# Three parts of queries and keys stored once, and read back for the stacks in three pieces instead of two

## The chip, the cores and the metric

The kernel runs on one core of one Trainium2 chip. The metric is the device time of the whole program in microseconds; the median of three runs is compared. Engines are called PE (matrix products), DVE (vector), ACT (scalar, activation functions), POOL (GpSimd) and SP (the queue that issues most DMAs).

## What is computed

A residual stream x of 2048 tokens by 128 channels passes a gated cumulative-sum block, then a two-layer feed-forward block with attention and experts, then a plain attention block, then the same feed-forward block once more:

```python
x = x + attn_a(layernorm(x), ...)
x = x + ffn(layernorm(x), ...)      # 2 layers: causal attention, then experts
x = x + attn_b(layernorm(x), ...)   # 16 heads of 8, no mask
x = x + ffn(layernorm(x), ...)      # the same weights again

# in ffn, for layer l in (0, 1):
x = x + attn(ln(x), wq[l], wk[l], wv[l], wo[l], ...)
x = x + moe(ln(x), ...)             # l == 0: two of eight experts by token; l == 1: two for the sequence
# attention of either kind
q, k, v = split into 16 heads of 8 columns
scores = q @ k.T * 8 ** -0.5        # causal in ffn
out = softmax(scores) @ v
```

So there are five attentions in the program. They are called f0 and f1 (the two layers of the first feed-forward block), b (the plain one), and g0 and g1 (the second feed-forward block); the last letter of a tile's name in the trace is f, b or g.

## The kernel before

**Stacks.** Every query and key value is split into three bf16 parts, high, mid and low (numbered 0, 1, 2), so that a product of two fp32 numbers becomes a sum of products of bf16 parts. Six such products are taken in one matmul, whose contraction runs over 48 rows: six groups of eight rows, one group for each product, eight rows for the eight columns of a head. `q_stack` holds on its partitions the parts 0, 1, 2, 0, 0, 1 of the queries and `k_stack` the parts 2, 1, 0, 0, 1, 0 of the keys; the upper half of the partitions holds the same for the odd heads. The parts are made with channels on partitions, so they pass through DRAM (`q_parts`, `k_parts`) to be regrouped.

**Writes.** The tokens are cut into four chunks of 512 columns (`CHUNKS`, c = 0 to 3). For each chunk SP writes three parts of q and of k. `Q_SLOTS` and `K_SLOTS` say which part stands in which of the four groups of DRAM rows; part 0 stands in two, so its write moves 256 KB and the other two move 128 KB. Each write adds 16 to `written[k][c % 2]`.

**Loads.** `load_stacks` (`EarlyProjection.load` in f1 and g1) loads chunk c for half b of the partitions. It waits until the three writes of q, then of k, have landed (`written` at 16 * 3 for each second chunk), and issues two DMAs for each stack: 32 rows, then 16 rows of the same DRAM tensor again. So one call issues four DMAs, and there are eight calls for each attention, 40 in all, 160 DMAs. Of one attention's eight calls, those of half 0 are issued by SP. Those of half 1 come from ACT for chunk 0 and from POOL for chunks 1 to 3 (in f1 and g1 SP issues the one of chunk 0 as well).

**Where the calls stand.** In f0 and b (`project_qkv`) and g0 (`project_behind`) the projection runs directly before the attention. SP writes the high parts of chunk c and then calls `load_stacks(sp, c - 1, 0)`; ACT makes the high parts of chunk 1 and then calls `load_stacks(act, 0, 1)`, ahead of copying a later chunk and of its mid parts:

```python
                    if c >= 2:
                        act.wait_ge(written[k][c % 2], 16 * 3 * (c // 2))
...
                if c == 1:
                    load_stacks(act, 0, 1)
                if c + 2 < CHUNKS:
                    copy_chunk(c + 2)
```

The first two of these lines let the high parts of chunk 3 be made only when the writes of chunk 1 have landed, since they share a buffer. In g0 POOL runs `load_stacks(pool, 1, 1)` and then `first_rows.powers(pool, BACK, 2)`, whose result `rstd` (line 848) DVE needs to normalise the last rows. In f1 and g1 (`EarlyProjection`) the projection of chunks 0 to 2 is spread through the experts of the layer before. There SP loads chunk 0 and half 0 of chunk 1 between rows of combine weights, and POOL loads half 1 of chunk 1 between its multiplications.

**In the attention.** PE, DVE, ACT and SP follow orders that `Plan` writes out ahead of time. PE scans scores for the row maxima (lines 1681 and 1692), DVE reduces them (1841, 1843, 1848), and SP sends the maxima as a shift row into `q_stack` (1913). PE then makes scores again (1719), ACT takes the exponential (1789), POOL sets what lies above the diagonal to zero in the causal layers (`affine_select`, 1902), and PE multiplies by the values (1740). POOL's loop over the diagonal units k holds the late loads: with `late` = 0 in f0 and g0, and 12 in f1 and g1, chunk 2 is loaded ahead of select number `late` and chunk 3 four selects later:

```python
                if (k - late) % 4 == 0 and 0 <= (k - late) // 4 < CHUNKS - EARLY:
                    projected["load"](pool, EARLY + (k - late) // 4, 1)
```

Of the kernel before, what the change touches and what calls it, by code (L numbers as in the profile page):

```python
# [7 lines left out]
BF16 = mybir.dt.bfloat16  # L8
# [8 lines left out]
S = 2048  # L17
# [18 lines left out]

Q_SLOTS = [0, 1, 2, 0]
K_SLOTS = [2, 1, 0, 0]
SLOTS = len(Q_SLOTS)
Q_AGAIN, K_AGAIN = 0, 1  # L40
AGAIN = 2
STACK = (SLOTS + AGAIN) * HD
PAIRS = HEADS // 2
# [34 lines left out]
class Memory:  # L78
# [35 lines left out]
    def __init__(self, nc, ctx, ins):  # L114
# [48 lines left out]
        self.weights_split = ctx.enter_context(nc.semaphore("weights_split"))  # L163
        self.q_dram = nc.dram_tensor("q_parts", [SLOTS * HD, HEADS, S], BF16, kind="Internal").ap()
        self.k_dram = nc.dram_tensor("k_parts", [SLOTS * HD, HEADS, S], BF16, kind="Internal").ap()
        self.r_dram = nc.dram_tensor("inverse_sums", [HEADS, S], F32, kind="Internal").ap()
# [450 lines left out]
def project_qkv(nc, m, n, buffers, first=None, layer=None):  # L617
# [6 lines left out]
    with ExitStack() as ctx:  # L624
# [34 lines left out]
        def write_part(sp, c, k, part):  # L659

            dram, parts_of = ((m.q_dram, Q_SLOTS), (m.k_dram, K_SLOTS))[k]
            places = [g for g, of in enumerate(parts_of) if of == part]
            stride = places[1] - places[0] if len(places) > 1 else 1
            dst = dram.rearrange("(g d) h q -> (d h) g q", d=HD)[:, places[0]:places[-1] + 1:stride,
                                                               c * CH:(c + 1) * CH]
            sp.dma_start(dst, parts[:, c % 2, k, part:part + 1, :].broadcast_to([P, len(places), CH]))\
                .then_inc(written[k][c % 2], 16)

        def load_stacks(queue, c, b):

            cols = slice(c * CH, (c + 1) * CH)
            for k, (stack, dram, arrived, again) in enumerate(((m.q_stack, m.q_dram, m.q_in, Q_AGAIN),
                                                               (m.k_stack, m.k_dram, m.k_in, K_AGAIN))):
                queue.wait_ge(written[k][c % 2], 16 * 3 * (c // 2 + 1))
                if c == CHUNKS - 1:
                    queue.wait_ge(v_ready, CHUNKS)
                at = HALF * b
                for n, first in ((SLOTS, 0), (AGAIN, again)):
                    queue.dma_start(stack[at:at + n * HD, c, :, :],
                                    dram.rearrange("r (hp b) s -> r b hp s", b=2)[first * HD:(first + n) * HD, b, :, cols])\  # L680
                        .then_inc(arrived[b][c], 16)
                    at += n * HD
# [208 lines left out]
def project_behind(nc, m, n, buffers, layer, first_rows, attended, finish):  # L891

    src, end = m.x, CHUNKS - 1
    with ExitStack() as ctx:
# [26 lines left out]
        def write_part(sp, c, k, part):  # L921

            dram, parts_of = ((m.q_dram, Q_SLOTS), (m.k_dram, K_SLOTS))[k]
            places = [g for g, of in enumerate(parts_of) if of == part]
            stride = places[1] - places[0] if len(places) > 1 else 1
            dst = dram.rearrange("(g d) h q -> (d h) g q", d=HD)[:, places[0]:places[-1] + 1:stride,
                                                               c * CH:(c + 1) * CH]
            sp.wait_ge((high_ready, mid_ready, low_ready)[part], 2 * c + k + 1)
            sp.dma_start(dst, parts[:, c % 2, k, part:part + 1, :].broadcast_to([P, len(places), CH]))\
                .then_inc(written[k][c % 2], 16)  # L930

        def load_stacks(queue, c, b):

            cols = slice(c * CH, (c + 1) * CH)
            for k, (stack, dram, arrived, again) in enumerate(((m.q_stack, m.q_dram, m.q_in, Q_AGAIN),
                                                               (m.k_stack, m.k_dram, m.k_in, K_AGAIN))):
                queue.wait_ge(written[k][c % 2], 16 * 3 * (c // 2 + 1))
                if c == end:
                    queue.wait_ge(v_ready, CHUNKS)
                at = HALF * b  # L940
                for n, first in ((SLOTS, 0), (AGAIN, again)):
                    queue.dma_start(stack[at:at + n * HD, c, :, :],
# [169 lines left out]
class EarlyProjection:  # L1112
# [105 lines left out]
    def write(self, sp, c, k, part):  # L1218
        sp.wait_ge((self.high_ready, self.mid_ready, self.low_ready)[part], 2 * c + k + 1)
        dram, parts_of = ((self.m.q_dram, Q_SLOTS), (self.m.k_dram, K_SLOTS))[k]  # L1220
        places = [g for g, of in enumerate(parts_of) if of == part]
# [5 lines left out]
    def load(self, queue, c, b):  # L1227
        m, cols = self.m, slice(c * CH, (c + 1) * CH)
        if c == 2:
            queue.wait_ge(*self.ones_back)  # L1230
        for k, (stack, dram, arrived, again) in enumerate(((m.q_stack, m.q_dram, m.q_in, Q_AGAIN),
                                                           (m.k_stack, m.k_dram, m.k_in, K_AGAIN))):
            queue.wait_ge(self.written[k][c % 2], 16 * 3 * (c // 2 + 1))
            at = HALF * b
            for n, first in ((SLOTS, 0), (AGAIN, again)):
                queue.dma_start(stack[at:at + n * HD, c, :, :],
# [388 lines left out]
def attention_heads(nc, m, n, buffers, projected, finish, rows_of, raw_weights, w2, stale, early, first_rows=None):  # L1625
# [8 lines left out]
    for g, (_, _, _, tiles) in enumerate(groups):  # L1634
        shift_moves.append((2 if tiles == TPC else 4) + (shift_moves[g - 2] if g >= 2 else 0))
    arrived = 32 * (m.layers + 1)
    m.layers += 1
# [1180 lines left out]
```

## Time and profile before

| what | value |
|---|---|
| median of three runs | 3050.44 us (3050.01 to 3052.54) |
| the profiled execution | 3052.74 us, of which the span of instructions is 3051.0 us |
| PE busy | 2639.0 us (86%) |
| DVE busy | 2597.2 us (85%) |
| ACT busy | 2249.0 us (74%) |
| POOL busy | 637.2 us (21%) |
| DMA | 109883 packets, 119.09 MB, mean 39 GB/s |

Busy time is time in instructions that compute. Issuing a DMA isn't counted as busy, though it holds the engine's queue, so an engine that issues DMAs shows as idle in this table. Each share is one of the whole span.

### The profile page before, as it was taken

How to read it: one execution, taken by the hardware profiler on the slowest of the kernel's cores; microseconds unless marked ns; L12 is line 12 of the kernel's file. 1: busy time of each engine (PE TensorE's matmuls, PEld its weight loads, DVE VectorE, ACT ScalarE, POOL GpSimd, SP SyncE). 2: the span in 40 equal slices, each digit the busy share in tenths (PEclk: the TensorE clock that was granted, in tenths of full speed). 3: DMA queues.
4: the chain of work that ended last, by engine and by line, in shares of the span. 5: the costliest groups of instructions: out<-in, count | busy, mean ns of one | idle time of the engine just before them, and what ended most of it. 6: DMA issues, size and time to landing. Idle time of an engine off the chain costs nothing. (4 is left out here: it accounts for less than half of the span.)

```text
span 3051.0 us, 71491 instructions
## 1 busy us (share of the span) xinstructions
PE 2639.0 (86%) x28144; PEld 1156.1 (38%) x28144; DVE 2597.2 (85%) x3516; ACT 2249.0 (74%) x4330; POOL 637.2 (21%) x1175
## 2 busy tenths in 40 slices
PE   3579999899799995779999999599999998899976
PEld 3432333677323333422222223233333775323325
DVE  4679999788799995799999999599998887899976
ACT  1248988677489884459999999478988675688874
POOL 5233211434421011100000000132102543321011
PEclk8779999999799997879999999799999998899998
DMA  1051000214300000320000000420001224300001
GB/s 34 29 125 36 27 25 18 66 54 102 71 24 22 14 13 26 78 63 9 15 12 13 12 15 10 119 54 27 16 13 32 64 63 94 62 31 16 13 16 28
DMA packets 109883, 119.09 MB, mean 39 GB/s; under 512 B 20726, under 2 KB 87660, under 8 KB 109548
## 3 DMA queue, kind: packets, MB, share of 16 engines
q1 hardware_dynamic: 102444, 98.21, 12.0%
q0 software_dynamic: 4608, 13.96, 2.2%
q8 instruction: 222, 3.64, 0.5%
q10 hardware_dynamic: 2496, 2.36, 0.4%
q14 instruction: 113, 0.93, 0.1%
HBM read 70.31 MB, written 43.78 MB: 37 GB/s over the span
## 5 line engine op out<-in xcount | busy, mean ns | idle before, releaser
L1789 ACT ACTIVATE h_probsf<-h_ps_lowf 128x512 f32<-128x512 f32 (+3 forms) x812 | 424.4, 550 | 111.5 <-PE h_ps_lowf L1719 70.9
L1789 ACT ACTIVATE h_probsg<-h_ps_lowg 128x512 f32<-128x512 f32 (+3 forms) x812 | 424.4, 550 | 104.1 <-PE h_ps_lowg L1719 65.7
L1789 ACT ACTIVATE h_probsb<-h_ps_lowb 128x512 f32<-128x512 f32 x683 | 389.1, 596 | 61.0 <-PE h_ps_lowb L1719 46.0
L1740 PE MATMUL h_ps_valuesf<-h_probsf,v_all 128*9 128x256 f32 (+2 forms) x4608 | 350.7, 377 | 25.9 <-POOL h_probsf L1902 19.2
L1740 PE MATMUL h_ps_valuesg<-h_probsg,v_all 128*9 128x256 f32 (+2 forms) x4608 | 348.3, 375 | 26.2 <-POOL h_probsg L1902 19.2
L1740 PE MATMUL h_ps_valuesb<-h_probsb,v_all 128*9 128x256 f32 x4096 | 317.9, 382 | 7.8 <-ACT h_drainedb L1798 3.1
L1841 DVE TENSOR_REDUCE h_maxima_0b<-h_ps_scanb 128x2 f32<-128x1024 f32 x256 | 292.7, 1216 | 6.6 <-PE h_ps_scanb L1681 6.4
L1841 DVE TENSOR_REDUCE h_maxima_2b<-h_ps_scanb 128x2 f32<-128x1024 f32 x256 | 292.8, 1217 | 5.1 <-PE h_ps_scanb L1681 5.1
L1841 DVE TENSOR_REDUCE h_maxima_0f<-h_ps_scanf 128x2 f32<-128x1024 f32 x224 | 258.8, 1217 | 19.2 <-PE h_ps_scanf L1681 18.6
L1841 DVE TENSOR_REDUCE h_maxima_0g<-h_ps_scang 128x2 f32<-128x1024 f32 x224 | 258.6, 1217 | 18.6 <-PE h_ps_scang L1681 17.9
L1789 ACT ACTIVATE h_probsf<-h_ps_highf 128x512 f32<-128x512 f32 (+3 forms) x404 | 224.0, 554 | 35.1 <-PE h_ps_lowf L1719 32.5
L1789 ACT ACTIVATE h_probsg<-h_ps_highg 128x512 f32<-128x512 f32 (+3 forms) x404 | 224.0, 554 | 35.0 <-PE h_ps_lowg L1719 32.3
L1902 POOL TENSOR_SCALAR_AFFINE_SELECT h_probsg<-h_probsg 128x128 f32<-128x128 f32 (+1 forms) x384 | 121.5, 330 | 608.9 <-ACT h_probsg L1789 601.8
L1681 PE MATMUL h_ps_scanf<-k_stack,q_stack 48*128 48x512 bf16 (+3 forms) x1280 | 218.8, 362 | 27.7 <-DVE h_maxima_0f L1841 8.2
L1902 POOL TENSOR_SCALAR_AFFINE_SELECT h_probsf<-h_probsf 128x128 f32<-128x128 f32 (+1 forms) x384 | 121.5, 330 | 577.8 <-ACT h_probsf L1789 571.0
L1681 PE MATMUL h_ps_scang<-k_stack,q_stack 48*128 48x512 bf16 (+3 forms) x1280 | 218.4, 361 | 24.0 <-DVE h_maxima_0g L1841 7.4
L1719 PE MATMUL h_ps_lowf<-q_stack,k_stack 49*128 49x256 bf16 (+2 forms) x1368 | 227.7, 286 | 11.4 <-DMA q_stack<-h_shiftsf 5.5
L1719 PE MATMUL h_ps_lowg<-q_stack,k_stack 49*128 49x256 bf16 (+2 forms) x1368 | 226.8, 286 | 7.4 <-ACT h_probsg L1789 2.6
L1681 PE MATMUL h_ps_scanb<-k_stack,q_stack 48*128 48x512 bf16 x1024 | 202.8, 393 | 21.5 <-DVE h_maxima_0b L1841 9.4
L1789 ACT ACTIVATE h_probsb<-h_ps_highb 128x512 f32<-128x512 f32 x341 | 203.4, 596 | 11.2 <-PE h_ps_lowb L1719 8.4
L1719 PE MATMUL h_ps_lowb<-q_stack,k_stack 49*128 49x256 bf16 x1366 | 200.4, 275 | 5.9 <-ACT h_probsb L1789 5.6
L1841 DVE TENSOR_REDUCE h_maxima_2f<-h_ps_scanf 128x2 f32<-128x1024 f32 x160 | 185.5, 1219 | 14.3 <-PE h_ps_scanf L1681 13.4
(478 smaller groups left out, 5226.7 us busy)
## 6 DMA issues: line engine op xcount, KB each, us to landing
q_stack<-combine_weights SPq DMA_DIRECT2D x64, 256.0 KB, 3.7
q_stack<-in_L_ffn_e_w SPq DMA_DIRECT2D x24, 256.0 KB, 3.4
q_stack<-q_parts SPq DMA_DIRECT2D x22, 256.0 KB, 5.6
k_stack<-k_parts SPq DMA_DIRECT2D x22, 256.0 KB, 7.4
attended<-h_drainedf SPq DMA_DIRECT2D x16, 256.0 KB, 2.3
attended<-h_drainedf SPq DMA_DIRECT2D x32, 128.0 KB, 2.0
attended<-h_drainedb SPq DMA_DIRECT2D x32, 128.0 KB, 1.9
attended<-h_drainedg SPq DMA_DIRECT2D x16, 256.0 KB, 2.5
```

The source lines that it names most:

```text
L1681: last = nc.tensor.matmul(ps_scan[:, i % RING_A, b, at:at + width], m.q_stack[rows, c, 2 * quad + hp, t * P:(t + 1) * P], m.k_stack[rows, ...
L1719: last[b] = nc.tensor.matmul(ps_scores[(2 * n_pair + b) % RING_S][:, width * i + off:width * (i + 1)], m.k_stack[rows, kb // TPC, pair, at ...
L1740: last = nc.tensor.matmul(ps_values[32 * j:32 * j + VD, low:high], m.v_all[:, kb, QUAD * quad + j, :], probs[:, (u + j % banks) % RING_P, ...
L1789: nc.scalar.activation(by_head(probs[:, of % RING_P, :], of), by_head(ps_scores[of % RING_S], of), ACT.Exp, scale=SOFTMAX_SCALE).then_inc( ...
L1841: nc.vector.tensor_reduce(found[:, :, low], now, AXIS_X, ALU.max).then_inc(freed, 1)
L1902: nc.gpsimd.affine_select(out=at, in_=at, compare_op=ALU.is_ge, fill=0.0, base=0, pattern=[[0, at.shape[1]], [1, P]], channel_multiplier=- ...
```

## The change

Each part is written to DRAM once: `q_parts` and `k_parts` have three groups of eight rows instead of four. The stacks, which hold the same as before, are read in three pieces of 24, 8 and 16 rows. The numbers for which the attention waits follow from the count of pieces (48 for each layer instead of 32).

```diff
-Q_SLOTS = [0, 1, 2, 0]
-K_SLOTS = [2, 1, 0, 0]
-SLOTS = len(Q_SLOTS)
-Q_AGAIN, K_AGAIN = 0, 1
-AGAIN = 2
-STACK = (SLOTS + AGAIN) * HD
+Q_PARTS = [0, 1, 2]
+K_PARTS = [2, 1, 0]
+PARTS = len(Q_PARTS)
+Q_ROWS = ((0, 3), (0, 1), (0, 2))
+K_ROWS = ((0, 3), (2, 1), (1, 2))
+STACK = sum(n for _, n in Q_ROWS) * HD
...
-        self.q_dram = nc.dram_tensor("q_parts", [SLOTS * HD, HEADS, S], BF16, kind="Internal").ap()
-        self.k_dram = nc.dram_tensor("k_parts", [SLOTS * HD, HEADS, S], BF16, kind="Internal").ap()
+        self.q_dram = nc.dram_tensor("q_parts", [PARTS * HD, HEADS, S], BF16, kind="Internal").ap()
+        self.k_dram = nc.dram_tensor("k_parts", [PARTS * HD, HEADS, S], BF16, kind="Internal").ap()
...
         def write_part(sp, c, k, part):
 
-            dram, parts_of = ((m.q_dram, Q_SLOTS), (m.k_dram, K_SLOTS))[k]
+            dram, parts_of = ((m.q_dram, Q_PARTS), (m.k_dram, K_PARTS))[k]
             places = [g for g, of in enumerate(parts_of) if of == part]
...
-                for n, first in ((SLOTS, 0), (AGAIN, again)):
+                for first, n in parts_of:
                     queue.dma_start(stack[at:at + n * HD, c, :, :],
                                     dram.rearrange("r (hp b) s -> r b hp s", b=2)[first * HD:(first + n) * HD, b, :, cols])\
                         .then_inc(arrived[b][c], 16)
...
-    arrived = 32 * (m.layers + 1)
+    arrived = 16 * len(Q_ROWS) * (m.layers + 1)
```

The write and the load are changed alike in the three places where they are written out. The order of PE's and DVE's instructions doesn't change. Three places on the other queues show what does.

On SP, in the projection of f0, before: the writes of chunk 1's high parts, the load of chunk 0's half 0, and the first mid part of chunk 1. `128x2x512` is a write to two places.

```order
L666 DMA q_parts<-p_partsf 128x2x512
L666 DMA k_parts<-p_partsf 128x2x512
L679 DMA q_stack<-q_parts 32x8x512
L679 DMA q_stack<-q_parts 16x8x512
L679 DMA k_stack<-k_parts 32x8x512
L679 DMA k_stack<-k_parts 16x8x512
L666 DMA q_parts<-p_partsf 128x512
```

The same place of the changed kernel:

```order
L666 DMA k_parts<-p_partsf 128x512
L679 DMA q_stack<-q_parts 24x8x512
L679 DMA q_stack<-q_parts 8x8x512
L679 DMA q_stack<-q_parts 16x8x512
L679 DMA k_stack<-k_parts 24x8x512
L679 DMA k_stack<-k_parts 8x8x512
L679 DMA k_stack<-k_parts 16x8x512
L666 DMA q_parts<-p_partsf 128x512
```

The writes keep their number and those of the high parts lose half of their size; four loads become six, ahead of the next writes.

On ACT, in the projection of b: the call for chunk 0's half 1, between the high parts of chunk 1 (815) and the copy of chunk 3 (801).

```order
 L815 ACTIVATE p_partsb<-p_ps_mixedb 128x512 x2
-L679 DMA q_stack<-q_parts 32x8x512
+L679 DMA q_stack<-q_parts 24x8x512
+L679 DMA q_stack<-q_parts 8x8x512
 L679 DMA q_stack<-q_parts 16x8x512
-L679 DMA k_stack<-k_parts 32x8x512
+L679 DMA k_stack<-k_parts 24x8x512
+L679 DMA k_stack<-k_parts 8x8x512
 L679 DMA k_stack<-k_parts 16x8x512
 L801 ACTIVATE q_stack<-p_ps_turnb 128x512
```

Two issues more stand ahead of the copy.

On POOL, in the attention of f1: the two late loads among the selects.

```order
 L1248 DMA k_stack<-k_stack 1x16x512 x2
 L1902 AFFINE_SELECT h_probsf<-h_probsf 128x128 x4
-L1236 DMA q_stack<-q_parts 32x8x512
-L1236 DMA q_stack<-q_parts 16x8x512
-L1236 DMA k_stack<-k_parts 32x8x512
+L1236 DMA q_stack<-q_parts 24x8x512
+L1236 DMA q_stack<-q_parts 8x8x512
+L1236 DMA q_stack<-q_parts 16x8x512
+L1236 DMA k_stack<-k_parts 24x8x512
+L1236 DMA k_stack<-k_parts 8x8x512
 L1236 DMA k_stack<-k_parts 16x8x512
 L1902 AFFINE_SELECT h_probsf<-h_probsf 128x128 x4
```

Each of the two calls has six issues where it had four, and the selects behind it stand behind them.

## Rows read from the trace of the kernel before

**Rows 1.** The page: the span.

```profile
span 3051.0 us, 71491 instructions
```

**Rows 2.** DMA issues: tile, queue, count, KB each, median us to landing.

```profile
q_stack<-q_parts SPq DMA_DIRECT2D x22, 256.0 KB, 5.6
...
q_stack<-q_parts POOLq DMA_DIRECT2D x15, 256.0 KB, 4.7
```

**Rows 3.** By source line: ns of one issue, min/median/max, first and last start.

```profile
L1236 SPq DMA_DIRECT2D k_stack<-k_parts x20: 591/602/617, 712.1 to 2625.2; - x20
...
L1236 POOL DMA_DIRECT2D k_stack<-k_parts x12: 530/558/583, 736.6 to 2607.5; - x12
...
L1248 POOL DMA_DIRECT2D k_stack<-k_stack x4: 507/544/584, 800.4 to 2599.5; - x4
```

**Rows 4.** Timeline of f0's start: start us, us, engine, line; idle before and releaser.

```profile
150.00 1.27 ACTq L679 DMA_DIRECT2D k_stack<-k_parts  x2
...
151.37 0.78 ACT L803 ACTIVATE q_stack<-p_ps_turnf,vecs 128x512 f32<-128x512 f32 x1 [3.87 <-issue]
...
160.28 1.26 ACT L818 ACTIVATE p_partsf<-p_ps_qkf,vecs_dh 128x512 bf16<-128x512 f32 x2 [3.35 <-DMA q_parts<-p_partsf]
...
164.81 0.61 PE L1681 MATMUL h_ps_scanf<-k_stack,q_stack 48*128 48x128 bf16 x4 [8.18 <-issue]
```

**Rows 5.** Windows: PE, PEld, DVE, ACT, POOL busy, PEclk, DMA share, GB/s.

```profile
152.00:162.00 10.00, 4.64 (x21) 3.35 (x19) 6.63 (x16) 5.08 (x10) 1.49 (x3) 0.84 1.00 229
```

**Rows 6.** Timeline of b's projection.

```profile
1278.22 0.60 ACT L801 ACTIVATE q_stack<-p_ps_turnb 128x512 f32<-128x512 f32 x1 [2.31 <-issue]
...
1279.36 1.29 DVE L755 TENSOR_TENSOR p_partsb<-p_restb,p_partsb 128x512 bf16<-128x512 f32 x2 [2.46 <-ACT p_partsb L826]
...
1288.01 0.60 ACT L815 ACTIVATE p_partsb<-p_ps_mixedb 128x512 bf16<-128x512 f32 x1 [2.63 <-PE p_ps_mixedb L789]
```

**Rows 7.** The chain that ended last, in g0's projection: start us, us, what.

```profile
1943.27 7.89 DMA q_parts<-p_partsg
...
1951.45 1.16 POOL q_stack L942 x2
1952.61 1.09 POOL k_stack L942 x2
...
1953.72 1.04 POOL rstd L848
```

**Rows 8.** Timelines of f1 and g1: value matmuls behind POOL's late loads.

```profile
807.33 0.41 PE L1740 MATMUL h_ps_valuesf<-h_probsf,v_all 128*9 128x128 f32 x8 [1.54 <-POOL h_probsf L1902]
...
810.59 1.04 PE L1740 MATMUL h_ps_valuesf<-h_probsf,v_all 128*9 128x256 f32 x8 [1.02 <-POOL h_probsf L1902]
...
2605.91 0.41 PE L1740 MATMUL h_ps_valuesg<-h_probsg,v_all 128*9 128x128 f32 x8 [1.52 <-POOL h_probsg L1902]
...
2609.18 1.04 PE L1740 MATMUL h_ps_valuesg<-h_probsg,v_all 128*9 128x256 f32 x8 [1.12 <-POOL h_probsg L1902]
```

**Rows 9.** Timeline of f0 behind POOL's second late load.

```profile
187.14 1.53 POOL L1902 TENSOR_SCALAR_AFFINE_SELECT h_probsf<-h_probsf 128x128 f32<-128x128 f32 x6
...
188.06 0.62 PE L1740 MATMUL h_ps_valuesf<-h_probsf,v_all 128*9 128x256 f32 x8
```

**Rows 10.** Timeline of the experts ahead of f1, behind POOL's load.

```profile
738.38 1.29 POOL L2312 TENSOR_TENSOR q_stack<-q_stack 128x512 f32<-128x512 f32 x1 [0.67 <-ACT q_stack L2643]
```

**Rows 11.** Timeline of f0: the first score matmul.

```profile
181.34 0.61 PE L1719 MATMUL h_ps_lowf<-q_stack,k_stack 49*128 49x512 bf16 x2 [4.15 <-DMA q_stack<-h_shiftsf]
```

**Rows 12.** DMA from 798 to 802 us: packets of SP's queue; issues.

```profile
q1 hardware_dynamic: 32, 0.00, 0.7%
...
q_stack<-h_shiftsf SPq DMA_DIRECT2D x2, 2.0 KB
```

**Rows 13.** Windows in f1, columns as in rows 5.

```profile
804.00:808.00 4.00, 2.46 (x41) 1.08 (x39) 2.00 (x4) 1.72 (x6) 3.99 (x10) 1.00 0.68 143
808.00:812.00 4.00, 2.60 (x34) 1.07 (x30) 2.44 (x2) 2.34 (x5) 2.93 (x9) 0.65 1.07 173
```

More of the change, by code:

```diff
@@ L671, in load_stacks @@
             cols = slice(c * CH, (c + 1) * CH)
-            for k, (stack, dram, arrived, again) in enumerate(((m.q_stack, m.q_dram, m.q_in, Q_AGAIN),
-                                                               (m.k_stack, m.k_dram, m.k_in, K_AGAIN))):
+            for k, (stack, dram, arrived, parts_of) in enumerate(((m.q_stack, m.q_dram, m.q_in, Q_ROWS),
+                                                               (m.k_stack, m.k_dram, m.k_in, K_ROWS))):
                 queue.wait_ge(written[k][c % 2], 16 * 3 * (c // 2 + 1))
@@ L921, in write_part @@
         def write_part(sp, c, k, part):
-            dram, parts_of = ((m.q_dram, Q_SLOTS), (m.k_dram, K_SLOTS))[k]
+            dram, parts_of = ((m.q_dram, Q_PARTS), (m.k_dram, K_PARTS))[k]
             places = [g for g, of in enumerate(parts_of) if of == part]
@@ L934, in load_stacks @@
             cols = slice(c * CH, (c + 1) * CH)
-            for k, (stack, dram, arrived, again) in enumerate(((m.q_stack, m.q_dram, m.q_in, Q_AGAIN),
-                                                               (m.k_stack, m.k_dram, m.k_in, K_AGAIN))):
+            for k, (stack, dram, arrived, parts_of) in enumerate(((m.q_stack, m.q_dram, m.q_in, Q_ROWS),
+                                                               (m.k_stack, m.k_dram, m.k_in, K_ROWS))):
                 queue.wait_ge(written[k][c % 2], 16 * 3 * (c // 2 + 1))
@@ L940, in load_stacks @@
                 at = HALF * b
-                for n, first in ((SLOTS, 0), (AGAIN, again)):
+                for first, n in parts_of:
                     queue.dma_start(stack[at:at + n * HD, c, :, :],
@@ L1219, in write @@
         sp.wait_ge((self.high_ready, self.mid_ready, self.low_ready)[part], 2 * c + k + 1)
-        dram, parts_of = ((self.m.q_dram, Q_SLOTS), (self.m.k_dram, K_SLOTS))[k]
+        dram, parts_of = ((self.m.q_dram, Q_PARTS), (self.m.k_dram, K_PARTS))[k]
         places = [g for g, of in enumerate(parts_of) if of == part]
@@ L1230, in load @@
             queue.wait_ge(*self.ones_back)
-        for k, (stack, dram, arrived, again) in enumerate(((m.q_stack, m.q_dram, m.q_in, Q_AGAIN),
-                                                           (m.k_stack, m.k_dram, m.k_in, K_AGAIN))):
+        for k, (stack, dram, arrived, parts_of) in enumerate(((m.q_stack, m.q_dram, m.q_in, Q_ROWS),
+                                                           (m.k_stack, m.k_dram, m.k_in, K_ROWS))):
             queue.wait_ge(self.written[k][c % 2], 16 * 3 * (c // 2 + 1))
             at = HALF * b
-            for n, first in ((SLOTS, 0), (AGAIN, again)):
+            for first, n in parts_of:
                 queue.dma_start(stack[at:at + n * HD, c, :, :],
```

## The prediction

> **What bounds the kernel now.** I read the span first [rows 1]: 3051.0 us, in a profiled execution of 3052.74 us, 1.7 us outside the span and 2.3 us above the median of 3050.44. The sum below is a difference; I make it against that execution and carry it to the median, so 3052.74 + d becomes 3050.44 + d. Then I looked for who issues the DMAs that the change touches and what one costs its engine: the list of DMA issues [rows 2] and the lines' durations [rows 3]. The reader is to see that an issue holds its queue for about 0.6 us on SP and 0.56 us on POOL, hardly spread over 20 and 12 cases that mix 32-row and 16-row loads. Then I read the timelines of the five starts of an attention, where little work is queued and each engine waits for the next [rows 4, 6, 11], the chain that ended last where it passes such a start [rows 7], and POOL's late loads, where PE waits [rows 8, 9]. In the middle of an attention the loads are long over; there the change has nothing to touch.
>
> **What is removed.** Each of the 40 high-part writes shrinks from 256 KB to 128 KB: two tensors by four chunks by five attentions, 5.2 MB in all. It can only help where the DMA queues are the limit. They are in the cold starts f0, b and g0: the share is 1.00 at 229 GB/s in f0 [rows 5]. Two releases hang on it. In f0 ACT waits 3.35 us for the writes of chunk 1 before it can make the high parts of chunk 3 [rows 4]. In g0 a DMA piece of 7.89 us ends in the release of POOL [rows 7]. Ahead of each such release stand the writes of chunk 0, the loads of chunk 0 and the writes of chunk 1 (1.05, 1.57 and 1.05 MB), of which 0.52 MB go. At 229 GB/s that is 2.3 us, the bound of the gain. In f0 no more than 3.35 - 1.25 = 2.1 us of it can be had, as ACT itself comes 1.25 us later (below).
>
> **How the packets are spread** decides how much of that arrives. The trace of before has no load of 8 or 24 rows. The nearest row is that of two shift DMAs of eight rows of 256 bytes: 32 packets for the two [rows 12], so eight with data and eight small ones for each, which fits eight DMA engines. If an 8-row load takes 8 engines and a 24-row load 12, both from the first one on, the fullest engine gets 16 + 8 + 8 = 32 packets of 1 KB for one stack where it had 16 + 8 = 24. Up to the release in f0 or g0 it then has 48 + 128 + 48 = 224 packets, against 64 + 96 + 64 = 224 before: no gain. The upper end of this term is a loss of 1.2 us, if two more SP issues ahead of chunk 1's mid and low writes show in full (2 x 0.60, [rows 3]). I take -0.5 us for each of f0 and g0, near the end for which the only row of a narrow DMA speaks, from a range of -2.1 (g0 -2.3) to +1.2. The Trainium skill, page "DMA: Bandwidth & Descriptors", section "Why a DMA increments its semaphore by 16 and not by 1", states this as a rule: a DMA runs on the largest number up to 16 that divides the slowest dimension of both sides, on the queues of SP and ACT always the lowest-numbered engines. The trace's eight small packets agree. With it both terms would be 0 and the time 1.0 us above mine; with an even spread they would be -2.1 and -2.3 and the time 3.4 us below.
>
> **What is added: 80 issues** (two for each of 40 calls), 44 on SP, 30 on POOL, 6 on ACT. What they hide behind differs by place.
>
> *SP.* In the experts 12 issues instead of 8 stand ahead of a row of combine weights, of which four are held ahead of POOL; in the attentions they stand behind a shift, and the next one waits for a whole group's search. Cost nothing; without that cover a call costs 1.2 us.
>
> *ACT, chunk 0.* Two issues take 1.27 us [rows 4], so two more 1.25 us. In f0 the copy behind them waited 3.87 us with nothing else shown as cause [rows 4], but ACT then has its 3.35 us of DMA wait: hidden, and already used above. In b the copy waits 2.31 us in the same way, DVE then 2.46 us for ACT's mid part, and the last high parts wait for PE, which waits for DVE, and not for a DMA [rows 6]. There nothing hides it: **b +1.25 us**, bounds 0 and 1.3. In g0 the same issues are over before the DMA piece of 7.89 us ends and POOL is released [rows 7], so they cost nothing there.
>
> *POOL in g0's projection.* Behind the DMA release the chain has POOL's four issues (1.16 + 1.09 us) and then the power for `rstd` [rows 7]. Two more issues at 0.56 [rows 3]: **g0 +1.1 us**. There is no engine beside it to hide them, since DVE's normalisation waits for `rstd`.
>
> *POOL's late loads, f1 and g1.* Each call is followed by selects for which PE waits: 1.54 and 1.02 us in f1, 1.52 and 1.12 in g1 [rows 8]. PE waits already, so each call's 1.1 us adds in full to its own stall, if the selects are what it waits for: **f1 and g1 +2.2 us each**, bounds 0 (DVE's search would be the limit behind it) and 2.2. PE's order is fixed, so scans stand behind the waiting value matmul and DVE runs dry with it.
>
> *POOL's late loads, f0 and g0.* The first call lies in the time before the first select. Behind the second one six selects take 1.53 us from 187.14, and PE takes the first four at 188.06 without a wait [rows 9], about when the fourth is done (187.14 + 4 x 0.255 = 188.16). 1.1 us later PE must wait: **f0 and g0 +1.0 us each** (g0 has the same order), bounds 0 and 1.1.
>
> *POOL in the experts ahead of f1 and g1.* The next multiplication starts after POOL has waited 0.67 us [rows 10]; 1.1 us more on POOL delays it by 0.4, and the power behind it, for which DVE waits. **+0.4 us each**, bounds 0 and 0.45. The DMA that spreads ones in the same code shows that POOL's cost doesn't hang on size: 544 ns for 16 KB against 558 [rows 3].
>
> **The sum.** f0: -0.5 + 1.0 = 0.5. f1: 0.4 + 2.2 = 2.6. b: 1.25. g0: -0.5 + 1.1 + 1.0 = 1.6. g1: 2.6. Together +8.55 us: 3052.74 becomes 3061.3 for a profiled execution, and the median 3050.44 + 8.55 = **3059.0 us**, 0.28% more. A change under 0.2% (6.1 us) can't be told from none in this kernel.
>
> **Rivals.** (1) *The late loads are partly covered.* After a POOL stall the search or the exponentials catch up, so that f1 and g1 lose one of their two calls, and f0's and g0's second call nothing: 8.55 - 2.2 - 2.0 = +4.35, **3054.8**. For it: DVE is 85% busy over the span and could be the limit soon after. Against it: PE waits at both calls, and the chain that ended last passes g1's POOL loads.
> (2) *Nothing added lies on the path; the bytes do.* This is the one that ends below. Issue time on ACT and POOL falls into waits that are there anyway, and the DMA queues give 2.1 us in f0 and 2.3 in g0: **3046.0**. It is decided by the issue terms: together they are 9.55 us here, and once more than 4.4 us of them reach the end it is no longer faster. Rows 7 and 8 speak against it.
> (3) *Narrow loads make the last data late, or PE's clock falls.* With the narrow spread and POOL's loads on the same first engines, a chunk puts 48 + 128 = 176 packets on the fullest one instead of 160, 10% more. In f0 the first score matmul waits 4.15 us for a shift DMA of eight rows on those same engines [rows 11]; a third more of load traffic ahead of it adds up to 1.4 us. In b chunks 2 and 3 arrive while DVE works through the scans, and up to 2 us of stall may show. Likewise for the clock: in f1 it was 1.00 until PE had been busy only 2.46 and 2.60 of 4 us around POOL's calls, then 0.65 [rows 13]; where f0 or g0 falls likewise, 4 us of PE work at half speed costs 2 us. Either adds about 3.5 to 4 us: **3063**. By the skill's rule named above it would come out so for the DMA half, on SP's and ACT's queues; what POOL's queue picks no row here shows.
>
> **How the numbers follow.** Forecast (3055.5 to 3062) 0.42, rival 1 (3052 to 3056.5) 0.23, rival 3 (3062 to 3068) 0.26, rival 2 0.09. The range from 3050.5 to 3067 leaves out rival 2 and the far end of rival 3. Slower by over 0.2% is above 3056.5: nearly all of the forecast (0.38), rival 3, and little of rival 1 (0.02), 0.66; within 0.2% 0.28; faster by over 0.2% (under 3044.3) would need rival 2 and more, or a stall of before that vanishes by chance: 0.06.
>
> **What would show it.** In g1 and f1 the two value matmuls behind POOL's late loads should wait 2.6 and 2.2 us; in f0 and g0 the one of rows 9 should wait about 1 us for a select. In b ACT's copy should wait 3.5 us with no releaser. In g0 the two POOL pieces of the chain should be 3.4 us long instead of 2.25. ACT's 3.35 us wait for a DMA in f0 should be about 1.6; 0 would mean an even spread. If the stalls in f1 and g1 are as long as I say and the time is not above 3056, rival 1 is right; if they aren't longer, POOL's issues cost less than 0.56 us for a narrow load, and the sum is wrong from its first step.

## The result

The changed kernel takes **3078.81 us** (median of four runs, 3075.46 to 3080.84) against 3050.65 us before: 28 us more by the medians. The ratio is 1.0083, with a 95% interval of 1.007 to 1.0095, so 25 us, from 21 to 29. The forecast was 8.55 us more, and the range ended at 3067.

The page of the changed kernel: the span, the packets, and the queues of SP (q1), POOL (q0) and ACT (q10) with packets, MB and share. The profiled execution took 3080.84 us.

```profile
span 3079.1 us, 71571 instructions
...
DMA packets 106404, 113.88 MB, mean 37 GB/s; under 512 B 22366, under 2 KB 84180, under 8 KB 106068
...
q1 hardware_dynamic: 97500, 92.96, 11.3%
q0 software_dynamic: 6048, 13.98, 2.4%
q10 hardware_dynamic: 2520, 2.36, 0.4%
```

5.2 MB have gone, as the change says, and the span is 28.1 us longer [rows 1]. Where they came in can be read from the same DVE instruction in both traces, the first and the last reduction of each attention's scans. All these are starts in us, and the last two columns differences of the stretch that ends there. `one_copy_16s` is the first experiment below.

| up to | before | changed | one_copy_16s | changed - before | changed - one_copy_16s |
|---|---|---|---|---|---|
| f0 first | 165.85 | 169.64 | 167.07 | +3.8 | +2.6 |
| f0 last | 521.54 | 522.07 | 517.90 | -3.3 | +1.6 |
| f1 first | 776.86 | 778.13 | 772.91 | +0.7 | +1.1 |
| f1 last | 1136.97 | 1143.41 | 1134.58 | +5.2 | +3.6 |
| b first | 1293.06 | 1301.04 | 1292.53 | +1.5 | -0.3 |
| b last | 1898.83 | 1912.20 | 1900.11 | +5.4 | +3.6 |
| g0 first | 1972.71 | 1988.02 | 1975.85 | +1.9 | +0.1 |
| g0 last | 2321.24 | 2341.33 | 2325.51 | +4.8 | +3.6 |
| g1 first | 2575.36 | 2597.03 | 2581.82 | +1.6 | -0.6 |
| g1 last | 2935.69 | 2962.26 | 2943.59 | +4.9 | +3.5 |
| end | 3047.60 | 3075.66 | 3057.13 | +1.5 | -0.1 |

So the loss isn't in the cold starts alone: each of the four later attentions is about 5 us longer. The rows that answer to those of before follow, first f1's value matmuls and POOL's late loads (timeline, as [rows 8]).

```profile
804.90 1.80 POOL L1236 DMA_DIRECT2D q_stack<-q_parts  x3 [0.29 <-issue]
806.69 1.73 POOL L1236 DMA_DIRECT2D k_stack<-k_parts  x3
...
809.50 0.41 PE L1740 MATMUL h_ps_valuesf<-h_probsf,v_all 128*9 128x128 f32 x8 [2.86 <-POOL h_probsf L1902]
...
814.00 1.04 PE L1740 MATMUL h_ps_valuesf<-h_probsf,v_all 128*9 128x256 f32 x8 [1.66 <-POOL h_probsf L1902]
```

The waits are 2.86 and 1.66 us where [rows 8] have 1.54 and 1.02. Next f0's start (as [rows 4, 11]), from the changed kernel's timeline.

```profile
154.29 0.78 ACT L803 ACTIVATE q_stack<-p_ps_turnf,vecs 128x512 f32<-128x512 f32 x1 [6.13 <-issue]
...
164.04 1.26 ACT L818 ACTIVATE p_partsf<-p_ps_qkf,vecs_dh 128x512 bf16<-128x512 f32 x2 [4.36 <-DMA q_parts<-p_partsf]
...
181.18 0.61 PE L1719 MATMUL h_ps_lowf<-q_stack,k_stack 49*128 49x512 bf16 x2 [0.20 <-DMA q_stack<-h_shiftsf]
```

ACT's wait for the writes of chunk 1 is longer, 4.36 instead of 3.35 us, not 1.6. But the first score matmul, which waited 4.15 us for a shift, waits 0.20 and starts at 181.18 instead of 181.34: what f0's projection lost, that wait absorbed. In b (timeline, as [rows 6]) it isn't absorbed:

```profile
1284.51 0.60 ACT L801 ACTIVATE q_stack<-p_ps_turnb 128x512 f32<-128x512 f32 x1 [3.79 <-PE p_ps_vb L781]
...
1285.65 1.29 DVE L755 TENSOR_TENSOR p_partsb<-p_restb,p_partsb 128x512 bf16<-128x512 f32 x2 [3.95 <-ACT p_partsb L826]
...
1287.66 3.68 PE L789 MATMUL p_ps_mixedb<-p_rawb,mix_dh 128*128 128x512 f32 x4 [3.83 <-DVE p_rawb L732]
...
1323.38 1.03 PE L1681 MATMUL h_ps_scanb<-k_stack,q_stack 48*128 48x512 bf16 x4 [5.75 <-DMA k_stack<-k_parts]
```

DVE waits 3.95 us for ACT where it waited 2.46, the four matmuls behind take 3.68 us, and then a scan waits **5.75 us for keys**. In the trace of before no scan matmul of b has a load as its releaser. One weight load has, and it stood idle hardly longer than the one ahead of it, 1.09 us against 1.03 (timeline of before):

```profile
1309.04 0.10 PEld L1681 LDWEIGHTS h_ps_scanb<-k_stack,q_stack 48*128 48x128 bf16 x2 [1.03 <-DVE h_maxima_2b L1841]
1310.24 0.13 PEld L1681 LDWEIGHTS h_ps_scanb<-k_stack,q_stack 48*128 48x128 bf16 x2 [1.09 <-DMA k_stack<-k_parts]
```

So the keys of b landed just when they were wanted already before the change, and there was next to no slack for a later load. Last g0's projection, the chain that ended last (as [rows 7]).

```profile
1951.47 0.80 ACTq L942
...
1955.14 0.59 ACTq L942
...
1957.98 7.84 DMA q_parts<-p_partsg
...
1966.11 0.68 POOL q_stack L942
...
1966.80 1.10 POOL q_stack L942 x2
1967.90 1.71 POOL k_stack L942 x3
```

The chain now passes ACT's six issues, 4.3 us from the first to the end of the last (1955.14 + 0.59 - 1951.47), ahead of the same DMA piece, and POOL's pieces are 3.5 us long.

### The profile page after: what moved, and what is told of

Same layout as the page of the kernel before. It is cut to its first block and busy times, and to the rows that moved or that the text cites. A ratio compares the mean times of both kernels' runs of the same rounds, so it can differ in the third digit from the quotient of the medians.

```text
span 3079.1 us, 71571 instructions
## 1 busy us (share of the span) xinstructions
PE 2654.8 (86%) x28144; PEld 1159.4 (38%) x28144; DVE 2600.4 (84%) x3516; ACT 2248.6 (73%) x4330; POOL 655.5 (21%) x1205
## 3 DMA queue, kind: packets, MB, share of 16 engines
q0 software_dynamic: 6048, 13.98, 2.4%
## 5 line engine op out<-in xcount | busy, mean ns | idle before, releaser
L1740 PE MATMUL h_ps_valuesg<-h_probsg,v_all 128*9 128x256 f32 (+2 forms) x4608 | 353.8, 380 | 28.1 <-POOL h_probsg L1902 20.9
```

Source lines behind the costliest of these rows:

```text
L1740: last = nc.tensor.matmul(ps_values[32 * j:32 * j + VD, low:high], m.v_all[:, kb, QUAD * quad + j, :], probs[:, (u + j % banks) % RING_P, ...
```

## The experiments

The change does three things at once: fewer bytes are written, a third issue is added to each stack, and loads of 24 and 8 rows take the place of loads of 32. Twelve runs take them apart, eleven of other kernels and one of the kernel before again, each timed in five rounds beside the kernel before. They ran in four groups, in which the median of the kernel before was 3051.82, 3051.47, 3053.77 and 3054.75 us; so kernels of one group are compared by their medians, and others by their ratios (0.001 is 3.05 us). The groups are those of the parts below: the first four, the next two with three_copies_one_load and three_q_two_k, then three_copies_16s, before_again and wide_in_b, and third_issue_on_pool by itself.

| kernel | parts written for q, k | pieces: SP and ACT / POOL | median us | ratio to before, 95% |
|---|---|---|---|---|
| before_again | 4, 4 | 32+16 / 32+16 | 3052.00 | 1.0003 (0.9986 to 1.002) |
| third_issue_on_pool | 4, 4 | 32+16 / 16+16+16 | 3058.87 | 1.0016 (1.0006 to 1.0025) |
| two_copies_16s | 4, 4 | 16+16+16 / the same | 3062.52 | 1.0029 (1.0018 to 1.0039) |
| one_copy_16s | 3, 3 | 16+16+16 / the same | 3062.78 | 1.0032 (1.002 to 1.0044) |
| three_q_two_k | 3, 4 | q 16+16+16, k 32+16 | 3063.22 | 1.0035 (1.0023 to 1.0048) |
| three_copies_one_load | 6, 6 | 48 / 48 | 3064.40 | 1.0040 (1.0025 to 1.0055) |
| narrow_in_b | 3, 3 | 16s, in b 24+8+16 | 3068.57 | 1.0044 (1.003 to 1.0057) |
| three_copies_16s | 6, 6 | 16+16+16 / the same | 3071.02 | 1.0058 (1.0045 to 1.0071) |
| narrow_on_pool | 4, 4 | 16s / 24+8+16 | 3071.10 | 1.0062 (1.0047 to 1.0076) |
| wide_in_b | 3, 3 | 24+8+16, in b 16s | 3075.49 | 1.0076 (1.0061 to 1.0091) |
| narrow_on_sp_act | 4, 4 | 24+8+16 / 16s | 3077.09 | 1.0080 (1.0067 to 1.0093) |
| the changed kernel | 3, 3 | 24+8+16 / the same | 3078.81 | 1.0083 (1.007 to 1.0095) |
| two_copies_24_8_16 | 4, 4 | 24+8+16 / the same | 3081.48 | 1.0093 (1.0078 to 1.0109) |

**Bytes, issues or width.** The first four kernels came together. The one copy can be read in runs of 16 rows if the parts stand in DRAM as 1, 0, 2, since then the pairs 1-0 and 0-2 cover all six products:

```diff
-Q_PARTS = [0, 1, 2]
-K_PARTS = [2, 1, 0]
-Q_ROWS = ((0, 3), (0, 1), (0, 2))
-K_ROWS = ((0, 3), (2, 1), (1, 2))
+Q_PARTS = [1, 0, 2]
+K_PARTS = [1, 0, 2]
+Q_ROWS = ((0, 2), (0, 2), (1, 2))
+K_ROWS = ((1, 2), (0, 2), (0, 2))
```

> Every part is still written once and each half of a stack still read in three runs, but the parts stand in DRAM as 1, 0, 2 for queries and for keys, so that all three runs are of 16 rows; the six products are the same, in another order down the rows. As many loads, bytes and issues as the changed kernel. Theory A (the 24- and 8-row loads of SP's and ACT's queue are served by 12 and 8 DMA engines, which makes the fullest engine carry 32 packets of a stack instead of 24): the scans of layer b no longer wait 5.75 us for the keys, and what is left is the cost of issues that was forecast, 3053 to 3061 us. Theory B (the third issue itself, on queues that are already late): nothing changes in that, 3074 to 3081 us. Theory C (fewer bytes written should have paid, and something in the single write costs): above 3061 us here, and not in the run with two copies.

With two copies, the tables of the kernel before (`[0, 1, 2, 0]`, `[2, 1, 0, 0]`) and rows `((0, 2), (2, 2), (0, 2))` and `((0, 2), (2, 2), (1, 2))`:

> The DRAM copies and writes of the kernel before (high parts twice), but the run of 32 rows is read as 16 and 16: only the issues are added, every load has 16 rows. Theory A: 3055 to 3062 us, my forecast of the issues' cost (+8.5 us) standing for itself. Theory B: 3074 to 3081 us. Theory C: as A.

The same tables with `((0, 3), (3, 1), (0, 2))` and `((0, 3), (3, 1), (1, 2))`:

> The DRAM copies and writes of the kernel before, read as 24, 8 and 16 rows: the loads of the changed kernel with the writes of the kernel before. Theory A: at or above the changed kernel, 3076 to 3088 us, since the narrow loads stay and more bytes are written beside them. Theory B: 3074 to 3081 us, the same as the run with 16, 16 and 16. Theory C: clearly below the changed kernel, 3055 to 3065 us.

one_copy_16s, with layer b's projection alone given the tables of the changed kernel:

> As the kernel with one copy and runs of 16 rows, but layer b alone keeps the order 0, 1, 2 and 2, 1, 0 and the runs of 24, 8 and 16 rows. Theory A: 6 to 9 us above the kernel with runs of 16 rows everywhere (layer b lost 8.6 us against the forecast 1.25), and a PE wait of 4 to 6 us for the keys early in b's scans; the other four attentions as in that kernel. Theory B: no difference between the two.

Theory A holds in these four. With the same writes, issues and bytes, 24+8+16 instead of 16+16+16 costs 3081.48 - 3062.52 = 19 us with two copies, and with one 1.0083 - 1.0032, 16 us. Theory B is out: a third issue of 16 rows brings 3062.5, not 3075. So is theory C: three or four parts written make no difference (3062.78 and 3062.52), so the 5.2 MB saved are worth nothing here that five rounds can tell. one_copy_16s came out 1.8 us above its band's top, two_copies_16s 0.5; narrow_in_b is 5.8 us above one_copy_16s by the medians (3.7 by the ratios), a little under the 6 that it was to have at least, and its keys wait 5.71 us as expected.

How many DMA engines a load uses can be inferred from packet counts. The pages' queue rows of the kernel before, of two_copies_16s and of two_copies_24_8_16, which write and read the same bytes:

```profile
q1 hardware_dynamic: 102444, 98.21, 12.0%
...
q10 hardware_dynamic: 2496, 2.36, 0.4%
```

```profile
q1 hardware_dynamic: 103148, 98.21, 12.4%
q0 software_dynamic: 5088, 13.97, 2.6%
...
q10 hardware_dynamic: 2592, 2.36, 0.5%
```

```profile
q1 hardware_dynamic: 102620, 98.21, 11.6%
q0 software_dynamic: 6048, 13.98, 2.4%
...
q10 hardware_dynamic: 2520, 2.36, 0.4%
```

SP loads 44 stacks. Its packets grow by 704 = 44 x 16 with the 16s: one more DMA, sixteen more small packets. With 24+8+16 they grow by 176 = 44 x 4, so the three pieces have 36 small packets where two wide ones have 32: 36 = 12 + 8 + 16. ACT's six stacks say the same, 96 = 6 x 16 and 24 = 6 x 4. If every engine that carries a load adds one small packet, the 24-row and the 8-row piece have 20 between them: 12 and 8, and eight small packets for eight rows is what the shift DMAs of [rows 12] had. No view names the engines themselves. In b less of the DMA engines' time is used with the narrow loads: the 12 us from ACT's first load on, first in two_copies_16s, then in two_copies_24_8_16 (windows, columns as [rows 5]).

```profile
1277.00:1289.00 12.00, 7.80 (x23) 3.76 (x22) 6.32 (x16) 3.43 (x7) 0.00 (x0) 0.86 0.97 192
```

```profile
1280.00:1292.00 12.00, 7.68 (x23) 3.75 (x22) 6.39 (x16) 3.30 (x7) 0.00 (x0) 0.86 0.84 175
```

0.97 of the engines' time was in use with the 16s and 0.84 with the narrow loads. The wait at the end of it is in the second kernel's timeline, and beside it what is left of it in one_copy_16s:

```profile
1326.19 1.04 PE L1681 MATMUL h_ps_scanb<-k_stack,q_stack 48*128 48x512 bf16 x4 [7.97 <-DMA k_stack<-k_parts]
```

```profile
1310.61 1.04 PE L1681 MATMUL h_ps_scanb<-k_stack,q_stack 48*128 48x512 bf16 x4 [1.49 <-DMA k_stack<-k_parts]
...
1319.96 1.11 PE L1681 MATMUL h_ps_scanb<-k_stack,q_stack 48*128 48x512 bf16 x4 [1.15 <-DMA k_stack<-k_parts]
```

**On which queue.** With two copies, the cut of the load was made to depend on the engine that issues it:

```diff
-                for first, n in parts_of:
+                for first, n in (NARROW_Q, NARROW_K)[k] if queue.engine == mybir.EngineType.Pool else parts_of:
```

with `NARROW_Q = ((0, 3), (3, 1), (0, 2))` and `NARROW_K = ((0, 3), (3, 1), (1, 2))`, and `!=` for the second kernel.

> As the kernel with two copies and runs of 16, 16 and 16 rows, but the loads that POOL issues are cut as 24, 8 and 16 rows. Theory A (the narrow spread over DMA engines costs, and it is that of SP's and ACT's queue): 3061 to 3066 us, at most 3 us above the kernel with 16s. Rival D (any cut that is not even costs, whatever the queue, since the three late POOL loads are the last of their stack): half or more of the 19 us between the two kernels with two copies, 3071 us or more.

> As the kernel with two copies and runs of 16, 16 and 16 rows, but the loads that SP and ACT issue are cut as 24, 8 and 16 rows. Theory A: nearly the whole of the loss, 3076 to 3082 us, with a scan of layer b waiting 4 us or more for keys. Rival D: 3062 to 3072 us.

By the ratios, SP's and ACT's narrow loads cost 1.0080 - 1.0029, 16 us over the 16s, as theory A had it. But POOL's alone cost 10 us, where A allowed 3: there rival D was right, and theory A fell as far as it spoke of SP's and ACT's queues alone. The two make 26 us together, against 19 for both at once. Four ratios stand in that difference, each with an interval of some 4 us to either side, so it doesn't show that the two losses overlap. The keys of b waited 7.82 us with SP's and ACT's narrow loads, and not at all with POOL's:

```profile
1319.62 1.03 PE L1683 MATMUL h_ps_scanb<-k_stack,q_stack 48*128 48x512 bf16 x4 [7.82 <-DMA k_stack<-k_parts]
```

(two lines were added at the head of that kernel, so 1683 is 1681). The traces tell the two queues apart by place. The same DVE instructions as in the table above give the length of each attention's scans, here in us more than before, from one trace of each kernel:

| trace | SP and ACT / POOL | f1 | b | g0 | g1 |
|---|---|---|---|---|---|
| one_copy_16s | 16s / 16s | 1.6 | 1.8 | 1.1 | 1.4 |
| two_copies_16s | 16s / 16s | 1.7 | 1.1 | 4.7 | 1.1 |
| narrow_in_b | 16s, in b narrow | 1.6 | 4.8 | 4.7 | 1.4 |
| narrow_on_sp_act | narrow / 16s | 1.6 | 8.0 | 2.2 | 1.4 |
| narrow_on_pool | 16s / narrow | 5.1 | 1.3 | 0.4 | 5.0 |
| two_copies_24_8_16 | narrow / narrow | 5.3 | 8.1 | 2.1 | 5.0 |
| the changed kernel | narrow / narrow | 5.2 | 5.4 | 4.8 | 4.9 |

b follows SP's and ACT's cut, f1 and g1 follow POOL's, and where both are narrow the two losses stand side by side in full. g0 follows neither: it is 4.7 us longer in two_copies_16s and in narrow_in_b as well, whose loads in g0 all have 16 rows, so the 3.6 us of g0 in the first table can't be put down to the narrow loads.

What POOL's narrow loads do stands in f1. The POOL and PE rows of one_copy_16s there, to be read against those of the changed kernel above:

```profile
799.98 1.61 POOL L1236 DMA_DIRECT2D q_stack<-q_parts  x3 [0.25 <-issue]
801.58 1.57 POOL L1236 DMA_DIRECT2D k_stack<-k_parts  x3
...
804.23 0.41 PE L1740 MATMUL h_ps_valuesf<-h_probsf,v_all 128*9 128x128 f32 x8 [2.47 <-POOL h_probsf L1902]
...
808.43 1.04 PE L1740 MATMUL h_ps_valuesf<-h_probsf,v_all 128*9 128x256 f32 x8 [1.54 <-POOL h_probsf L1902]
```

Three narrow issues take 1.80 and 1.73 us, three of 16 rows 1.61 and 1.57, so the stall behind them is 0.4 and 0.1 us shorter with the 16s. That is small; but TensorE's granted clock is lower too. In the 24 us from POOL's first late load on it was 0.86 of full speed in one_copy_16s and 0.79 in the changed kernel (windows, which start where that load does in each):

```profile
800.00:824.00 24.00, 17.77 (x208) 6.14 (x204) 15.46 (x18) 13.17 (x36) 15.53 (x46) 0.86 0.63 96
```

```profile
805.00:829.00 24.00, 17.96 (x192) 6.06 (x192) 14.12 (x17) 12.64 (x34) 15.56 (x44) 0.79 0.49 89
```

The same stretch has 0.86 in narrow_on_sp_act too, and 0.79 and 0.61 in the two other kernels of the table with narrow loads on POOL. Of the 3.6 us between the changed kernel and one_copy_16s in f1, 1.0 has come 15 us behind the late loads and 2.1 after 50 us; the other 1.5 come in one step some 100 us later, where the changed kernel's clock drops (the row of 902 us at the end) and that of one_copy_16s doesn't. So most of the loss in f1 isn't in the stall itself, and it stands where the granted clock is lower. No run holds the clock fixed, so that the clock is its cause is argued and not shown.

**Layer b alone.** The changed kernel with the order 1, 0, 2 and the 16s in b only:

> The changed kernel, but layer b has the parts in the order 1, 0, 2 and loads of 16, 16 and 16 rows; the four others keep 24, 8 and 16. By narrow_in_b (5.8 us above one_copy_16s by the medians, the interval reaching from 1 to 8) 3 to 8 us below the changed kernel: 3070 to 3076 us, and no wait of more than 2 us for keys in the scans of b. If the narrow loads in b only moved a loss that comes anyway: 3077 to 3080 us.

The ratio is 1.0076, 2 us under the changed kernel's 1.0083, and the intervals overlap, so the time alone decides nothing; by the medians, each against its own group's, it is 6 us. The longest wait for keys in b's scans is down to 1.31 us. With narrow_in_b (+5.8) and the first table (3.6 us in b) it says that b's narrow loads cost some 2 to 6 us. As much again or more lies in f1 and g1 (3.6 and 3.5 us in the first table). The trace of wide_in_b is of its fastest run, 3064.84 us, 10.6 under its median, and there f1 and g1 are only 2.9 and 2.4 us longer than before, with narrow loads on POOL: their loss differs between executions.

**What the issues cost.** Three kernels asked for it at other counts. All six products written out, so that a stack is one load:

```diff
-Q_PARTS = [0, 1, 2]
-K_PARTS = [2, 1, 0]
-Q_ROWS = ((0, 3), (0, 1), (0, 2))
-K_ROWS = ((0, 3), (2, 1), (1, 2))
+Q_PARTS = [0, 0, 0, 2, 1, 1]
+K_PARTS = [2, 0, 1, 0, 1, 0]
+Q_ROWS = ((0, 6),)
+K_ROWS = ((0, 6),)
```

> The opposite of the change: all six rows of products stand in DRAM (queries 0, 0, 0, 2, 1, 1, keys 2, 0, 1, 0, 1, 0), the high part written three times and the mid part twice, 384 KB of a stack against 512 KB each for queries and keys of a chunk becoming 768 KB, and each half of a stack is one load of 48 rows. If a load's issue costs as the runs so far say (one more each cost 9 to 10 us over the kernel before), one less gives 6 to 11 us back: 3041 to 3046 us. Rival E (bytes on the path of the loads): the 50% more written delays the chunks in b and g0, where DMA is busy 1.0 of the time, by 2 us each, and eats half or all of it: 3047 to 3056 us.

(The sizes in this text are garbled: a chunk's writes for q and k together go from 1.05 MB, eight parts of 128 KB, to 1.57 MB, twelve parts.)

The same tables with rows `((0, 2), (2, 2), (4, 2))`:

> The writes of the kernel with three copies (six parts' worth written for each stack instead of four or three), read in three runs of 16 rows, so that only the number of issues, six instead of two, stands between them. If an issue costs about 4 to 5 us over the kernel, as one more on top of the kernel before seemed to (9 to 10 us for two to three), and the written bytes ate the gain of the single load: 3074 to 3086 us. If issues cost little and every kernel that is not the one before is 10 us longer for another reason: 3062 to 3068 us, as with one load.

And `Q_PARTS = [1, 0, 2]`, `K_PARTS = [0, 2, 1, 0]` with q rows `((0, 2), (0, 2), (1, 2))` and k rows `((0, 4), (2, 2))`:

> Queries written once and read in three runs of 16 rows, keys with the high part twice and read as 32 and 16 rows (products in the order 1-0, 0-2, 1-1, 0-0, 0-1, 2-0): five issues for the two stacks of a load instead of six or four, all of them of 16 or 32 rows. If the cost goes with the count of issues: about half of the 10 us of the kernels with 16s, 3054 to 3059 us. Rival F (the cost is that of queries alone, whose loads come first, so that keys behind them cost nothing more): as with 16s for both, 3060 to 3064 us.

At twelve parts, six issues instead of two cost 1.0058 - 1.0040, 5.5 us, between the two cases that I had set; with the intervals of both ratios that may be nearly nothing or twice as much. And the single load, at 3064.4 us, is slower than even rival E allowed. It gains nothing on the kernel before: by the next comparison the bytes take more than it gives; in b its scans wait for keys as well, though no load of it is narrow.

```profile
1316.02 1.03 PE L1681 MATMUL h_ps_scanb<-k_stack,q_stack 48*128 48x512 bf16 x4 [4.24 <-DMA k_stack<-k_parts]
```

Against two_copies_16s, three_copies_16s costs 1.0058 - 1.0029, 9 us, for 50% more parts. So written bytes are free from three to four parts for each tensor, and not from four to six. three_q_two_k, with five issues, is no cheaper than with six, as rival F had it; whether F's reason holds no run tells. Its trace has the loss in another place: a scan of b waits 4.14 us for keys, and b is 3.7 us longer than before, against 1.8 in one_copy_16s, though its loads have 16 and 32 rows. In three_copies_16s that wait is 2.93 us.

```profile
1314.08 1.04 PE L1680 MATMUL h_ps_scanb<-k_stack,q_stack 48*128 48x512 bf16 x4 [4.14 <-DMA k_stack<-k_parts]
```

So narrow loads are not the only thing that makes b's keys late.

The last kernel is the one before with only POOL's loads cut in 16s:

> The kernel before with two copies and loads of 32 and 16 rows on SP and ACT as they were; only the loads that POOL issues are cut as 16, 16 and 16 rows, 30 issues more instead of 80. My forecast put 8.3 of its 9.55 us of issue terms on POOL (f0 1.0, f1 2.6, g0 2.1, g1 2.6) and 1.25 on ACT in b: by it 3058 to 3061 us, and value matmuls in f1 that wait 2.5 and 1.6 us. Rival: the 10 us of the kernels with 16s come as much from SP's and ACT's third issue, which delays writes and so the data of b (keys awaited 2.6 us there with one copy): 3055 to 3058 us.

The median lies in the band of my forecast, but the kernel before was 3054.75 us in this group; the ratio of 1.0016 is +4.9 us (1.8 to 7.6), and that is the rival's size. The waits are as said, 2.50 and 1.56 us in f1. So POOL's 30 issues may carry about half of the 9 us of two_copies_16s, and SP's and ACT's 50 the other half; the intervals of the two ratios leave room for other shares.

**The kernel before, again.**

> The kernel before itself, for a second profile of it. Theory G (its trace of 3052.74 us had luck with TensorE's clock: no drop in mid-attention, where the traces of all the other kernels have one to five of some 1.2 us each): a second trace shows one to four such drops, and its time is within 0.1% of the kernel before. Against it: again none, so that the drops belong to the other kernels.

The time is the same. One of its twelve runs took 3078.44 us, with a granted clock of 0.888 over the whole run, where the eleven others had 0.938 to 0.941 and ended by 3056.04. In its trace the clock drops once in mid-attention, where that of before held it; the two windows, first before, then before_again:

```profile
2834.00:2838.00 4.00, 3.56 (x40) 1.08 (x40) 4.00 (x5) 3.43 (x7) 0.00 (x0) 1.00 0.10 33
```

```profile
2834.00:2838.00 4.00, 3.65 (x34) 0.83 (x34) 4.00 (x4) 3.43 (x7) 0.00 (x0) 0.77 0.10 33
```

One drop in mid-attention is within the one to four that theory G asked for, and one_copy_16s has this one too, so before's trace had some luck. But it explains 0.9 us of g1, and 2.7 us of the whole trace, and not the 28.

## Why the prediction was wrong

**The step that failed** is the one on how the packets are spread. It had the mechanism right: 12 and 8 engines, 32 packets on the fullest one for a stack instead of 24. It then counted packets only up to the two releases in f0 and g0, found 224 against 224, and set the term to "no gain". What a third more on the fullest engine does to every load behind those releases was left to rival 3, with "up to 2 us of stall" in b and a total of 3.5 to 4. The runs put 16 to 19 us on the narrow cut: scans of b wait 5.75 us for keys, or 7.97 with two copies, and with 16s in their place 1.5 or less. The count up to the release was a count of the wrong thing for b, because what its scans wait for is a load behind it. An estimate for b: its ten stacks on SP's and ACT's queues put 8 packets more each on the fullest engine, 80 of 1 KB, and at a sixteenth of the 229 GB/s of [rows 5] these take 5.7 us; the longest wait for keys grew by 4.2 us from one_copy_16s to narrow_in_b, and by 7.3 from two_copies_16s to two_copies_24_8_16. POOL's narrow loads had no term at all, as no row showed what its queue picks, and they cost 10 us; beside two_copies_16s the trace of narrow_on_pool has f1 3.4 and g1 3.9 us longer, with no scan that waits for keys. That "the change has nothing to touch" in the middle of an attention failed with it: 1.5 us of f1's loss came there, at a clock drop. The Trainium skill, page "DMA: Bandwidth & Descriptors", section "Why a DMA increments its semaphore by 16 and not by 1", gives the number of engines as the largest up to 16 that divides the slowest dimension of both sides; the packet counts agree for SP and ACT (36 = 12 + 8 + 16).

**The terms of the sum.** Their total, +8.55, may be held against the kernels with the 16s, where only issues are added: +8.9 and +9.8 us by the ratios. The total was right and its parts weren't, so that is luck.
- *Late loads, f1 and g1* (2.2 each): the waits in f1 were to be 2.6 and 2.2 us. In one_copy_16s they are 2.47 and 1.54, so they grew by 0.93 and 0.52 instead of 1.1 and 1.1. By the table its f1 and g1 are 1.6 and 1.4 us longer than before, not 2.2; and of that 1.3 us each come in one step at a clock drop some 230 us behind the late loads. At the loads themselves 1.2 us appear in both, of which 0.3 and 0.2 are left 50 us later. So for the cost of the third issue there, rival 1 ("partly covered") was nearer than the forecast.
- *b* (+1.25): DVE's wait for ACT grew by 1.49, about as said. But four matmuls behind it took 3.68 us where the same four took 1.99, at a granted clock of 0.66 of full speed from 1287 to 1292 us, and in one_copy_16s 3.53, so that comes with the third issue and not with the narrow cut. And the keys came late. In the changed kernel the stretch up to b's first reduction and b itself cost 1.5 + 5.4.
- *g0* (ACT's issues "cost nothing there"): in the changed kernel the chain passes all six, where before it passed none. POOL's two pieces are 3.5 us long, for which 3.4 was forecast.
- *f0* (-0.5): ACT's wait grew to 4.36 where 1.6 was forecast. It cost nothing, since the shift wait of 4.15 us took it all; 1.0 for the second late load didn't show either, as the value matmuls there wait no longer for a select than before.
- *Bytes*: nothing between three and four parts, as the -0.5 said nearly.

On POOL the forecast had 8.3 of 9.55 us, and its third issue measures 4.9 (1.8 to 7.6). By the difference, SP's issues in the projections and experts, which I had costed at nothing, together with ACT's would make up the rest; which of them, no run tells.

**Still open**: how much of the 3.6 and 3.5 us in f1 and g1 is TensorE's clock; why g0 is 4.7 us longer in some kernels and 1.1 or less in others with the same loads there; and why the keys of b come late with five issues of 16 and 32 rows.

## What to carry to other kernels

Where a layout gives pieces of 24 and 8 rows, ask first whether another order of the groups gives 16 and 16, on every queue that issues them: here it costs no byte and brings back 16 us, and with two copies the narrow cut cost 16 us on SP's and ACT's queues and 10 on POOL's. Count what the fullest DMA engine carries up to the last load that somebody waits for, not up to the first. Compare windows of two traces from the same instruction on, not at the same time. And hold a saving in bytes against the places where a load is awaited: between three and four parts written it was worth nothing, while from four to six parts bytes cost 9 us.

## What the hardware did that I had not expected

- The issue of a narrow load takes longer on its engine: SP's medians by line were 0.65 to 0.71 us in the changed kernel and 0.60 with the 16s, POOL's three 1.80 us against 1.61.
- On POOL's queue a narrow stack has more packets, not fewer: 6048 against 5088 over 30 stacks, 32 more for each.
- A clock drop of TensorE in mid-attention, 0.57 in the first row below, comes and goes between kernels whose code there is the same, and DVE falls behind by 1.2 to 1.5 us at each. PE was busy nearly all of these 4 us. The changed kernel's windows show five of them, two in f1, two in g0 and one in g1; those of 1042, 2242 and 2862 us are in one_copy_16s too, those of 902 and 2102 are not:

```profile
902.00:906.00 4.00, 3.94 (x32) 0.63 (x32) 2.39 (x3) 2.45 (x6) 0.00 (x0) 0.57 0.18 66
1042.00:1046.00 4.00, 3.97 (x32) 0.86 (x30) 3.50 (x4) 2.49 (x7) 0.00 (x0) 0.57 0.10 33
2102.00:2106.00 4.00, 4.00 (x40) 0.72 (x36) 3.35 (x3) 2.99 (x7) 0.00 (x0) 0.80 0.08 31
2242.00:2246.00 4.00, 4.00 (x46) 1.02 (x42) 3.34 (x4) 3.21 (x6) 0.00 (x0) 0.81 0.00 0
2862.00:2866.00 4.00, 4.00 (x39) 1.04 (x35) 3.27 (x3) 2.41 (x6) 0.00 (x0) 0.66 0.09 32
```
